# Cross-attention of a decoder layer: where in a step the row maxima are transposed, and when they are copied out

## The reference

```
def _L0_xattn_ref(q, k, v, gamma):        # q = x after the first layer norm, k = v = ctx_2048
    N_HEAD = 8                            # B, Dq, Lq = 32, 128, 512; dq = 16
    qh = q.reshape(B, h, dq, Lq); kh = k.reshape(B, h, dq, Lk); vh = v.reshape(B, h, dv, Lk)
    qk = jnp.einsum('bhdq,bhdl->bhql', qh, kh) / sqrt(dq)
    sm = jax.nn.softmax(qk, axis=-1)
    ret = jnp.einsum('bhql,bhdl->bhdq', sm, vh)
    return gamma * ret.reshape(B, Dv, Lq)
```

## Time and profile before

| | |
|---|---|
| median of three runs | 1811.45 us |
| the profiled execution: its own time | 1802.17 us |
| its span, first to last instruction | 1800.3 us |
| mean granted clock of TensorE | 0.945 of full |
| TensorE busy (matmuls) | 1611.2 us, 90% of the span |
| VectorE busy | 1521.2 us, 84% |
| ScalarE busy | 1328.8 us, 74% |
| GpSimd busy | 1092.0 us, 61% |
| costliest group in the stage: row maxima, VectorE, line 969 | 620.6 us, 512 of 1224 ns |
| exponentials, ScalarE, line 945 | 555.9 us, 1024 of 599 ns |
| score tiles, products, units on TensorE, lines 1077, 1059, 1029 | 327.6, 316.0, 280.9 us |

### The profile page before, as it was taken

One profiled execution on the slowest core, in us unless ns is written; L12 is line 12 of the kernel. 1 busy time (PEld: TensorE's weight loads), 2 busy tenths in 40 slices (PEclk: granted clock), 3 DMA queues, 4 the chain that ended last, 5 costly groups with the idle time before them and its releaser, 6 DMA issues. The chain is left out here.

```text
span 1800.3 us, 35221 instructions
## 1 busy us (share of the span) xinstructions
PE 1611.2 (90%) x12000; PEld 873.2 (49%) x12000; DVE 1521.2 (84%) x1894; ACT 1328.8 (74%) x2821; POOL 1092.0 (61%) x1532
## 2 busy tenths in 40 slices
PE   6999999999998798999999999999867877778764
PEld 5777777777776333333333333333323333333332
DVE  5778787888787897999999999999568898988885
ACT  4666555454545387888888888888778888888993
POOL 6667676766766442355553555423467888888872
PEclk9999999999998798999999999999978888888897
DMA  4455434343446454444555554445333333333311
GB/s 144 144 177 175 136 107 135 106 130 117 120 126 169 117 99 114 120 109 120 125 158 156 160 131 116 111 120 127 94 114 91 113 104 116 106 106 112 106 53 41
DMA packets 119269, 217.10 MB, mean 121 GB/s; under 512 B 32241, under 2 KB 34705, under 8 KB 116785
## 3 DMA queue, kind: packets, MB, share of 16 engines
q1 hardware_dynamic: 110770, 213.64, 41.7%
q0 software_dynamic: 8320, 1.21, 0.4%
HBM read 137.67 MB, written 76.02 MB: 119 GB/s over the span
## 5 line engine op out<-in xcount | busy, mean ns | idle before, releaser
L969 DVE TENSOR_REDUCE b_smax<-wide 128x2 f32<-128x1024 f32 x512 | 620.6, 1224 | 46.3 <-PE wide L1029 33.4
L945 ACT ACTIVATE b_prob<-bank 128x512 f32<-128x512 f32 x1024 | 555.9, 599 | 96.7 <-PE bank L1077 90.8
L1077 PE MATMUL bank<-b_xs,b_cs 50*128 50x512 f32 x1024 | 327.6, 476 | 12.4 <-DMA b_xs<-b_max_part 11.4
L1059 PE MATMUL sums<-b_prob,b_vT 128*32 128x256 f32 (+1 forms) x3584 | 316.0, 424 | 5.6 <-ACT b_prob L945 0.5
L1029 PE MATMUL wide<-b_cs,b_xs 48*128 48x512 f32 x1024 | 280.9, 435 | 8.8 <-DVE b_smax L969 7.3
L1077 PEld LDWEIGHTS bank<-b_xs,b_cs 50*128 50x128 f32 x1024 | 132.9, 186 | 220.0 <-ACT b_prob L945 167.8
L885 POOL TENSOR_SCALAR b_max_part<-b_neg_max 16x128 fp32r<-16x128 f32 x64 | 18.4, 288 | 303.1 <-ACT b_neg_max L936 302.4
L370 ACT ACTIVATE a_prob<-wide,a_neg_max 128x128 f32<-128x128 f32 x512 | 181.5, 418 | 2.5 <-DVE a_neg_max L461 2.5
L1987 PE MATMUL wide<-c_w,c_xqT 128*128 128x512 bf16 x512 | 166.5, 498 | 0.0
L895 POOL DMA_DIRECT2D b_xs<-b_max_part x256 | 133.6, 527 | 42.1 <-POOL b_max_part L888 37.3
L1059 PEld LDWEIGHTS sums<-b_prob,b_vT 128*32 128x32 f32 x3584 | 72.7, 108 | 163.3 <-issue 96.9
(11 more groups left out here) (156 smaller groups left out, 3351.6 us busy)
## 6 DMA issues: line engine op xcount, KB each, us to landing
scratch_c_part<-a_c_part SPq DMA_DIRECT2D x64, 256.0 KB
scratch_x_part<-a_x_part SPq DMA_DIRECT2D x64, 256.0 KB
b_xs<-scratch_x_part SPq DMA_DIRECT2D x128, 128.0 KB, 3.1
b_cs<-scratch_c_part SPq DMA_DIRECT2D x128, 128.0 KB, 3.1
scratch_heads<-b_heads SPq DMA_DIRECT2D x64, 256.0 KB, 2.9
a_xT<-in_xT SPq DMA_DIRECT2D x32, 256.0 KB, 6.4
a_c_in<-in_ctx SPq DMA_DIRECT2D x32, 256.0 KB, 2.6
a_x<-in_x SPq DMA_DIRECT2D x32, 256.0 KB, 4.2
```

The lines of the kernel that those rows point to most:

```text
L945: act.activation(prob[k % 8][:, :], e_ps[bank_of(UNITS * t + k)][:, :], ACT.Exp, scale=0.25).then_inc(exp_done, 1)
L969: dve.tensor_reduce(smax[g][:, :, j, qc], m_ps[u % 2][:, :, :], AX.X, ALU.max, negate=True).then_inc(max_done, 1)
L1059: last = pe.matmul(av_ps[2 * XD * h:2 * XD * (h + 1), cols], vT[p][:, lc, XG * g + h, :], prob[(XG * n + 2 * j + e) % 8][:, cols], start=( ...
L1077: pe.matmul(e_ps[bank_of(UNITS * t + 2 * u + e)][:, :], cs[p][g][half(e), j, lc * P:(lc + 1) * P], xs[p][g][half(e), j, :], start=True, st ...
```

## The change

The transposition goes to the first bank of `m_ps[1]` instead of `m_ps[0]`. TensorE issues it in the middle of sub-step 0 or 4, behind products part 0 and ahead of the second half's first score tile; it waits for units 0 to 7 (or 8 to 15) to be reduced and for none of the next half. The unit that waits for the copy is now unit 1 or unit 9, which is in the same sub-step, right behind one score tile. ScalarE copies behind the second exponential of sub-step 0 or 4. In the run-up (`begin`), the same move is made by one unit.

```
             if not first:
                 act.wait_ge(part_done, 4 * b + 2 * g - 2)
-            act.activation(neg_max[g][:, :], m_ps[0][0:XG * KC, 0, 0:P], ACT.Copy).then_inc(neg_done, 1)
+            act.activation(neg_max[g][:, :], m_ps[1][0:XG * KC, 0, 0:P], ACT.Copy).then_inc(neg_done, 1)
...
                     act.activation(prob[k % 8][:, :], e_ps[bank_of(UNITS * t + k)][:, :], ACT.Exp, scale=0.25).then_inc(
                         exp_done, 1)
+                    if j == 1 and n == 0:
+                        evict_max(t, 1, first=first)
+                    if j == 1 and n == 4 and not last:
+                        evict_max(t + 1, 0)
                     if j == 0 and n == 1 and not first:
                         copy_heads(t - 1, 1, first=second)
                     if j == 0 and n == 5:
                         copy_heads(t, 0, first=first)
-                if n == 0:
-                    evict_max(t, 1, first=first)
-                if n == 4 and not last:
-                    evict_max(t + 1, 0)
...
             pe.wait_ge(max_done, beside)
-            pe.transpose(m_ps[0][0:XG * KC, 0, 0:P], smax[g][:, :, :, :].rearrange("p e b c -> p (e b c)"),
+            pe.transpose(m_ps[1][0:XG * KC, 0, 0:P], smax[g][:, :, :, :].rearrange("p e b c -> p (e b c)"),
                          ident[:, :]).then_inc(mt_done, 1)
...
             for n in range(STEPS):
                 score(s, p, 2 * n, (0, 1), first)
-                for j in range(2):
-                    if not last:
-                        u = 2 * n + j
-                        max_unit(*after(s, p), u, after_mt={2: 2 * t + 2, 10: 2 * t + 3}.get(u))
-                    if j == 0:
-                        attended(n, 0)
-                    score(s, p, 2 * n + 1, (j,), first)
+                if not last:
+                    max_unit(*after(s, p), 2 * n)
+                attended(n, 0)
+
+                if n == 0:
+                    transpose_max(s, p, 1, PAIRS * (t + 1))
+                if n == 4 and not last:
+                    transpose_max(*after(s, p), 0, PAIRS * (t + 1) + 8)
+                score(s, p, 2 * n + 1, (0,), first)
+                if not last:
+                    max_unit(*after(s, p), 2 * n + 1, after_mt={1: 2 * t + 2, 9: 2 * t + 3}.get(2 * n + 1))
+                score(s, p, 2 * n + 1, (1,), first)
                 attended(n, 1)
-                if n == 0:
-                    transpose_max(s, p, 1, PAIRS * (t + 1) + (0 if last else 1))
-                if n == 4 and not last:
-                    transpose_max(*after(s, p), 0, PAIRS * (t + 1) + 9)
...
             while u < to:
-                max_unit(0, 0, u, first=True, after_mt=1 if u == 10 else None)
-                if u == 9:
-                    transpose_max(0, 0, 0, 9)
+                max_unit(0, 0, u, first=True, after_mt=1 if u == 9 else None)
+                if u == 8:
+                    transpose_max(0, 0, 0, 8)
                 u += 1
```

## The result

The changed kernel takes 1837.88 us (median of four runs, 1837.17 to 1849.44), the kernel before 1814.83 us (median of four). The ratio is **1.014, 95% interval 1.0097 to 1.0183**: slower by 25 us, 18 to 33. The forecast was 1834 us in a range of 1808 to 1848, with +24.8 us as its sum.

What follows compares the result with a forecast made beforehand. The prediction took TensorE to set the pace. +30.4 us for the new wait and -5.6 us for earlier small transfers gave +24.8 us, from which it took 1834 us, in a range of 1808 to 1848 us.

Steps and rivals of the forecast that it cites:

- Who sets the pace: Steady cross-attention step: TensorE, not VectorE, sets the pace; VectorE's 16 units need 18.1 of 20.85 us.
- The old wait: Unit 2 or 10 no longer waits for the maxima's copy; worth nothing, since the heads' copy wait covers it.
- rival 1: Sub-steps n = 1 and 5: the heads' wait, 0.44 us, absorbs the new one; 1809 us, chance 12%.
- The new wait: Unit 1 or 9 waits for the maxima's copy, delaying what is queued behind: 0.49 us per half-step, +30.4 us.
- Rival 3: Last score tile runs beside the first, ahead of the waiting unit; loss partly absorbed, 1817 us, chance 8%.
- rival 4: Unit 3 waits for unit 1's reduction, or lower activity costs granted clock; 1854 us, chance 8%.
- The transfers: Small transfers of the maxima start earlier, with 1.72 us more slack, shortening TensorE's waits: -5.6 us, bounds 0 and -13.
- The sum: Whole kernel: +30.4 us of new wait less 5.6 us of transfers gives +24.8 us.

Runs made afterwards that it cites:

- run 1: Changed kernel with each row maximum taken over only 256 of 512 columns, about halving VectorE's reduction time: 1840.72 us, ratio 1.0149.
- run 6: Kernel before, with the third score tile issued ahead of unit 2 or 10 at n = 1 and 5: 1818.87 us, ratio 1.0011.
- run 4: Kernel before, with ScalarE's heads' copy put ahead of the first exponential of sub-steps 1 and 5: 1818.27 us, ratio 1.0036.
- run 7: Kernel before, with the heads' copy made by VectorE instead of ScalarE, except in the last step: 1803.86 us, ratio 0.9935.
- run 3: Changed kernel, with the last score tile of sub-steps 0 and 4 issued ahead of the waiting unit: 1827.63 us, ratio 1.0076.
- run 5: Changed kernel, with the transposition ahead of products part 0 and the copy behind the first exponential: 1817.78 us, ratio 1.0016.
- run 8: Changed kernel, with one more small ScalarE copy between transposition and copy of the maxima: 1857.95 us, ratio 1.0269.
- run 9: As run 7, with VectorE's reciprocals moved from sub-step 5 to sub-step 7: 1855.72 us, ratio 1.0231.
- run 10: As run 9, with VectorE's reciprocals in sub-step 6 instead of 7: 1801.53 us, ratio 0.9931.
- run 11: The kernel of run 7 measured again, beside run 10: 1808.68 us, ratio 0.9964.
- run 2: Changed kernel, with the maxima copied behind the third exponential of sub-steps 0 and 4 instead of the second: 2015.72 us, ratio 1.1118.

## Why the prediction was right

*Who sets the pace.* TensorE, as read from the 1.13 us between reductions against the recorded 1.22. Run 1 shows it directly.

*The old wait.* Forecast at nothing; run 6 had a score tile run in its time and gained nothing. The reason given was incomplete. The products of n = 1 were said to be free at 3.99 but for the heads' copy. Runs 4 and 7 put the floor at 4.27 to 4.29 (in run 7 they start 1.62 behind their pair): the last score tile waits for an exponential of its own sub-step. So the slack that rival 1 counted on was 0.16 us, not 0.44, and in run 4 the expectation that rested on it failed. The next pair has a cover of its own besides. It starts 0.17 us behind the exponential that frees its bank: in the kernel before, the second of the three exponentials from 1152.49 on ends at 1152.49 + 0.49 + 0.60 = 1153.58, and the pair's weights load at 1153.75.

```profile
1152.49 1.59 ACT L945 ACTIVATE b_prob<-bank 128x512 f32<-128x512 f32 x3
1153.75 0.18 PEld L1077 LDWEIGHTS bank<-b_xs,b_cs 50*128 50x128 f32 x2 [0.84 <-ACT b_prob L945]
```

*The new wait.* Forecast 0.49 us a half-step (the prediction's own times, 3.15 - 2.67, give 0.48); measured 0.52 (2.67 to 3.19) and about 1.05 us a step, 62 x 0.52 = 32 us in place of 30.4. The difference is the last score tile, 0.35 behind the unit and not 0.31. Runs 3, 5 and 8 change only what stands between the transposition and the unit, or behind it, and the pair-to-pair time followed by 0.24, 0.40 and 0.20 us. Rival 1 falls with the 2.77 us of n = 1, where it needed 2.4. Rival 3 falls with the order of the loads: the last score tile's weights were loaded at 1180.20, behind those of the waiting unit at 1180.06, and its matmul stood behind the unit's.

```profile
1180.20 0.19 PEld L1077 LDWEIGHTS bank<-b_xs,b_cs 50*128 50x128 f32 x1
```

That is the row's reading, by which the prediction went, and not what it had worked out from the Trainium skill, *TensorE: Matmul & The Clock Gate*, section "The mechanism". Of rival 4, one half did not come: unit 3 loads at 1181.91, 0.05 us behind the end of unit 1's reduction (1180.63 + 1.23) and without a recorded wait. The other half, that granted clock is lost, came at the start of the stage, as follows.

*The transfers.* Forecast -5.6 us, bounds 0 and -13. The three steps of the earlier trace rows at full clock lost their waits; two short ones of some 0.5 and 0.6 us are left in other steps. With those of before that were too short to be counted, that is about -3.4. The long step fell from 27.03 us, 6.2 over the undisturbed one, to 24.58, 2.7 over: -3.5 where -1.7 was forecast. But the step behind it took 34.78 us at a granted clock of 0.52 where it had been 23.91 at 0.83: in this execution TensorE stayed at the lower level for some 34 us after a shorter idle time. The prediction took it that a shorter wait could only help the clock behind it, and the other traces speak against that. Counted from transposition to transposition, the half-step behind the one with the longest wait ran at a mean granted clock of 0.50, 0.50, 0.68, 0.72 and 0.58 in the five traces with the transposition in its new bank (the changed kernel, runs 1, 3, 5, 8), and of 0.74 to 0.99 in the seven without (the kernel before, runs 4, 6, 7, 9, 10, 11), although the wait of the matmuls ahead of it was 1.5 to 4.1 us in the first and 3.5 to 5.8 in the second. The disturbed half-steps at this place together stood 6.6 to 15.6 us over undisturbed ones in the first, 5.8 to 9.2 in the second. So the waits for the transfers did get shorter, but that this saved time here is not shown.

*The sum.* +24.8 was forecast, 25 (18 to 33) measured. That the two agree so closely is in part luck. The new wait, 32 us, is shown step by step; the other -7 lies inside what the interval leaves (-14 to +1), and no run measures it by itself. The transfers' term of -5.6 may stand for it or not. In the two profiled executions it went the other way: from the first transposition to the last they took 672.84 and 709.50 us, 36.7 apart, which is the 32 and some 5 us more of disturbed half-steps.

*Left open.* Why the clock stays low for longer behind a shorter wait (34 us in one execution against 10 before) was not tried; nor from which wait between those of runs 8 and 2 on the clock falls.

## What to carry to other kernels

In this kernel a transposition that goes round by ScalarE takes about 0.7 us from its issue to the next use of its bank. What it costs depends on how much of TensorE's own list lies between the two, and on what is queued behind the waiting instruction. Before removing a wait, look at the next ones in the same list: here TensorE's wait for the maxima was covered by later waits for ScalarE, and moving it forward put it where nothing covered it. A recorded busy share near full says little; the distance between starts in a stretch where the engine runs back to back says whether it sets the pace, and whether it can take over work, as VectorE did in run 10. And a sum that agrees with a median does not show its terms: each has to be found in the trace.

## What the runs showed of the hardware that was not expected

- Idle times of 0.93 us ahead of the matmuls of one unit, twice in a step, took the mean granted clock of the stage to 0.78 (run 2), and added some 120 us to the 57 that the waits themselves cost. With 0.2 us more than the changed kernel's wait (run 8) an undisturbed step stayed at full clock.
- A shorter idle time was followed by a longer stretch at the lower clock: 17.9 us at 0.50 behind a wait of 2.7 us (the changed kernel; run 1 the same behind 2.6), 11.95 us at 0.81 behind one of 5.8 us (the kernel before).
- A 0.24 us instruction of VectorE's waited up to 5.0 us for a GpSimd instruction that no semaphore joins it to (run 9, eight times). In the profile it shows as a long duration, not as a wait.
